# Gram matmuls of a half chunk in two blocks of two PSUM banks, and the last layer in four column tiles

## The reference

```python
e = jnp.stack([tbl_0[ids[:, 0]], ..., tbl_26[ids[:, 26]]], axis=1)    # 2048 x 27 x 128
dot_products = jnp.einsum('bnd,bmd->bnm', e, e)
z = dot_products[:, c, r]                                             # pairs below the diagonal: 351
h = jnp.concatenate([z, dense_ctx], axis=1)                           # 367
h = jnp.maximum(h @ W_top1 + b_top1, 0.0)                             # 512
h = jnp.maximum(h @ W_top2 + b_top2, 0.0)                             # 256
y = h @ W_top3                                                        # 1
```

## Time and profile before

| | us |
|---|---|
| median of 3 runs | 572.7 |
| lowest, highest | 572.4, 577.95 |
| the profiled execution | 572.74 |
| its span in the trace (first to last instruction) | 570.9 |
| mean TensorE clock granted, share of full | 0.848 |
| PE busy, PEld busy | 419.2, 367.1 |
| DVE, ACT, POOL busy | 232.5, 147.5, 253.0 |

### The profile page before, as it was taken

The page is one execution under the profiler, slowest core; times in us unless marked ns, Lnnn a source line. Parts: engine busy times, 40 slices in busy tenths (PEclk is TensorE's granted clock), DMA queues, the critical chain, the costliest instruction groups (busy, mean ns, idle before and its releaser), DMA issues.

```text
span 570.9 us, 10250 instructions
## 1 busy us (share of the span) xinstructions
PE 419.2 (73%) x4118; PEld 367.1 (64%) x4118; DVE 232.5 (41%) x730; ACT 147.5 (26%) x310; POOL 253.0 (44%) x269
## 2 busy tenths in 40 slices
PE   3411567867786896779896887858978688689887
PEld 3311566846775785658684775747867587578676
DVE  6511685524562262532462433433336225354200
ACT  3210241212221331223121331222312223124542
POOL 6777454446554443642545336254444453450000
PEclk9755588869797896978788898787979789799998
DMA  8943261234223421413215132052211431133130
GB/s 202 230 119 86 74 202 33 84 79 105 60 78 90 86 60 28 127 45 77 64 29 148 26 77 68 22 139 47 77 36 52 120 82 55 38 100 66 37 68 1
DMA packets 69280, 45.97 MB, mean 81 GB/s; under 512 B 53443, under 2 KB 57795, under 8 KB 69233
## 3 DMA queue, kind: packets, MB, share of 16 engines
q1 hardware_dynamic: 59255, 27.82, 20.4%
q0 software_dynamic: 8384, 17.19, 11.6%
q10 hardware_dynamic: 1594, 0.31, 0.3%
HBM read 39.53 MB, written 5.76 MB: 79 GB/s over the span
## 4 chain that ended last, share of the span: by engine, by line
PE 63%; issue 14%; another core or an unknown queue 11%; DVE 6%; DMA 2%; ACT 2%; SPq 1%; ACTq 0%; DVEq 0%
PE lookup_ps L558 33%; PE gram_ps L587 13%; PE layer_ps L604 7%; PE gather_ps L543 5%; DVE one_hot L833 5%; PE layer_ps L616 4%; PE layer_ps L624 1%; DMA ids_all<-lookup_ids 1%; DVE table_lo L840 1%; DMA emb<-tbl 1%; ACT z L735 1%; DMA z<-gram_dram 1%; SPq L357 1%; ACT h_rest L735 0%
## 5 line engine op out<-in xcount | busy, mean ns | idle before, releaser
L511 POOL DMA_INDIRECT rows<-tbl,index x256 | 246.4, 962 | 256.3 <-PE gather_ps L543 160.8
L833 DVE TENSOR_SCALAR one_hot<-ids_all,row_number 125x256 fp32r<-125x256 int32 x688 | 208.3, 366 | 295.0 <-remote 151.7
L558 PE MATMUL lookup_ps<-one_hot,table_hi 125*128 125x256 f32 x680 | 208.9, 332 | 86.3 <-issue 43.0
L558 PEld LDWEIGHTS lookup_ps<-one_hot,table_hi 125*128 125x128 f32 x680 | 145.6, 214 | 100.4 <-issue 65.0
L558 PE MATMUL lookup_ps<-one_hot,table_lo 125*128 125x256 f32 x680 | 193.7, 309 | 17.0 <-issue 16.7
L558 PEld LDWEIGHTS lookup_ps<-one_hot,table_lo 125*128 125x128 f32 x680 | 146.9, 216 | 26.4 <-issue 26.1
L587 PE MATMUL gram_ps<-emb 128*52 128x54 f32 x2048 | 84.4, 231 | 37.7 <-issue 35.4
L587 PEld LDWEIGHTS gram_ps<-emb 128*52 128x52 f32 x2048 | 69.8, 142 | 54.0 <-issue 47.2
L330 ACT COPY gram<-gram_ps 128x432 f32<-128x432 f32 x64 | 33.2, 518 | 193.9 <-remote 161.8
L697 ACT ACTIVATE emb<-lookup_ps 128x256 f32<-128x256 f32 x85 | 35.0, 412 | 83.8 <-remote 40.8
L686 ACT ACTIVATE emb<-gather_ps 128x512 f32<-128x512 f32 x64 | 38.9, 608 | 63.7 <-PE gather_ps L543 46.4
(11 more groups left out here) (40 smaller groups left out, 107.5 us busy)
## 6 DMA issues: line engine op xcount, KB each, us to landing
ids_all<-lookup_ids SPq DMA_DIRECT2D x43, 256.0 KB
gram_dram<-gram SPq DMA_DIRECT2D x62, 87.8 KB
emb<-tbl SPq DMA_DIRECT2D x11, 448.0 KB
rows<-tbl,index POOLq DMA_INDIRECT x256
z<-gram_dram SPq DMA_DIRECT2D x14, 117.0 KB
ids_all<-lookup_ids SPq DMA_DIRECT2D x7, 128.0 KB
z<-gram_dram SPq DMA_DIRECT2D x7, 91.0 KB
emb<-w SPq DMA_DIRECT2D x3, 192.0 KB
```

Of the source, the lines that this page charges most:

```text
L511: pool.indirect_dma_start(rows[k][:, j * DIM:(j + 1) * DIM], None, tables[f], bass.IndirectOffsetOnAxis(index[p][:, h, f:f + 1], 0)).then_ ...
L558: last = nc.tensor.matmul(lookup_ps[lookup_bank(c, p, k)], table[:, k, row, :], one_hot[u % UNIT_RING][:, r, :], start=(row == 0 and table ...
L833: last = nc.vector.tensor_scalar(one_hot[u % UNIT_RING][:, r, :], table_ids, row_number[0:LOOKUP_PARTS, row:row + 1], None, ALU.is_equal)
```

## The change

The four gram banks of a half are no longer spread singly, but in two blocks of two. A block stands at one position. `last_order()` is left as it is.

Layer three splits its 256 samples into four lots of 64. Each lot is a matmul of its own with the same weight column, and its output goes to another column tile (PSUM partitions 0, 32, 64 and 96, columns 0 to 63 of the bank). So there are eight fp32 matmuls (16 instructions) of 64 columns in place of two (four instructions) of 256. ACT's copy takes all 128 partitions by 64 columns, in place of one by 256, and the store reads four partitions of it.

```diff
+def by_blocks(events, first, end):
+
+    starts = spread([events[n:n + GRAM_BANKS] for n in range(0, len(events), GRAM_BANKS)], first, end)
+    return [(at, event) for at, block in starts for event in block]
@@ half_order
     if h == 1:
         return merged(spread([("unit", c + 1, u) for u in range(EARLY_UNITS)]), spread(gathers_of(c, 1), offset=0.6),
-                      spread(grams_of(c, 0), GRAMS_FROM, GRAMS_TO[h]))
+                      by_blocks(grams_of(c, 0), GRAMS_FROM, GRAMS_TO[h]))
     events = [spread([("unit", c, u) for u in range(EARLY_UNITS, N_UNITS)]), spread(gathers_of(c, 0), offset=0.6),
-              spread(grams_of(c - 1, 1), GRAMS_FROM, GRAMS_TO[h])]
+              by_blocks(grams_of(c - 1, 1), GRAMS_FROM, GRAMS_TO[h])]
@@ dlrm_tower
+        Y_TILES = 4
+        Y_COLS, Y_STEP = CHUNK // Y_TILES, P // Y_TILES
@@ tower
-            return Tower(z_sb, h1_sb, [h2_one, h1_sb[0]], h1_more[0:1, 0, :])
+            return Tower(z_sb, h1_sb, [h2_one, h1_sb[0]], h1_more[:, 0, 0:Y_COLS])
@@ layer3
                     pe.wait_ge(h2_ready, c * o2_tiles + k + 1)
-                    last = nc.tensor.matmul(layer_ps[0][0:1, 0:CHUNK], w3_sb[:, k:k + 1], to.h2[k],
-                                            start=(k == 0), stop=(k == o2_tiles - 1))
+                    for j in range(Y_TILES):
+                        last = nc.tensor.matmul(layer_ps[0][j * Y_STEP:j * Y_STEP + 1, 0:Y_COLS], w3_sb[:, k:k + 1],
+                                                to.h2[k][:, j * Y_COLS:(j + 1) * Y_COLS],
+                                                start=(k == 0), stop=(k == o2_tiles - 1))
                 last.then_inc(l3_full, 1)
@@ copy_y
-                nc.scalar.activation(to.y, layer_ps[0][0:1, 0:CHUNK], ACT.Copy).then_inc(y_ready, 1)
+                nc.scalar.activation(to.y, layer_ps[0][:, 0:Y_COLS], ACT.Copy).then_inc(y_ready, 1)
...
-                act.dma_start(y_out[bass.ds(c * CHUNK, CHUNK), :].rearrange("b o -> o b"),
-                              to.y).then_inc(y_stored, 16)
+                act.dma_start(y_out[bass.ds(c * CHUNK, CHUNK), :].rearrange("(j b) o -> j (b o)", j=Y_TILES),
+                              to.y[0:P:Y_STEP, :]).then_inc(y_stored, 16)
```

## The result

The changed kernel took 598.15 us (median of 4 runs, 595.98 to 599.98). The kernel before, run beside it, took 575.09 (572.4 to 577.95). The ratio is 1.040, with an interval of 1.032 to 1.048: slower by 4%, where 565.1 was forecast and 582 was the upper end of the range.

The account below looks back on a forecast made before the run. PE bounds the kernel, standing in windows of gather calls. From 572.74: odd `h == 1` +16.65, even -1.5, `h == 0` -21.3, last `h == 0` -0.8, first `h == 1` -0.3, end -0.35; together -7.6, 565.1 us; range 553 to 582.

Parts of the forecast that it names:

- the windows: Time from POOL's first gather call on: PE runs normally a while, then nearly stands until 1.0 to 2.1 us after the last.
- `h == 1` of the odd chunks: g3 to g7: blocks stand in g3's window and in the joined windows of g5 and g6; 5.55 us longer, three times.
- the even halves: `h == 1` of even chunks, g3 to g7: g4's calls stay late, 8.6 us after g3; 0.5 us shorter, three times.
- `h == 0`: g7 to L1: g7 comes when its window is over; 4.0 and 3.1 us shorter, three times each, and 0.8 at the last.
- the prediction's own list of what would make it wrong: g4's even-half signal in time (5 us lost each, three times), smaller window allowance for dense blocks, or units waiting for DVE.
- The block behind g1: Second block of `h == 0`, 18.1 to 19.9 us after g7: passes as a window opens, units behind stand, L1 at 23.75.
- Rival C: The `h == 0` block at the opening window stands in its middle: 2.85 us more in six halves, 582 us; chance 0.25.
- what a window lets through: In POOL's call windows PE first passes 48 to 52 matmuls at normal pace; grams inside a window bring the stand.
- Rival D: Stands depend on the DMAs alone, not the grams, so their sum stays; switches and layer three go: 564.7 us; chance 0.08.
- Layer three: 16 quarter-width matmuls on PE take 0.45 us where four took 0.95; 0.5 us saved each time.
- the row taken: Gram bank in the trace, two tiles of 54 columns at 28 ns a matmul, used to cost layer three at 0.45 us.
- Its store: Layer three's store, four rows of 256 bytes for one of 1 KB: costs nothing, perhaps some tenths at the end.

Follow-up runs that it names:

- the first run: The kernel before with the gram blocks alone, layer three, its copy and store as before: 594.65 us, ratio 1.029, chip P.
- the half-by-half runs: Layer three in tiles, chip R, against the kernel before: blocks in `h == 0` alone 570.18 us, ratio 1.020; in `h == 1` alone 589.54 us, 1.054.

## Why the prediction was wrong

**Right: the windows and what they do in `h == 1` of the odd chunks.** The odd timeline was forecast with g4 at 3.9 after g3, the block at 6.3, done at 14.2, g5 16.95, g6 20.7, second block 22.2, g7 34.9. Measured in chunk 3: 3.8, 6.1, 14.9, 17.2, 20.8, 22.3, 34.9. Chunks 3 and 5 lost 5.5 and 6.2 us (forecast 5.55). Blocks outside windows are 1.76 us (forecast 1.75).

**Wrong, the largest: the even halves.** They were to gain 0.5 us each, since the prediction kept the late calls of g4 (8.6 us after g3 on the chain) as they were in the kernel before, though its own shorter layer three moved g4. In the kernel before, g4's signal comes 2.8 us after the gather's end (209.30 for 206.52). In the changed kernel it comes 1.5 us after it (219.44 for 217.93) and was out before the block began at 219.74. The place of the banks is not what makes the difference. With layer three in tiles and a single bank one unit behind g4, as in the kernel before (tiles alone, and blocks in `h == 0` alone), g4 ends 4.4 us after the start of g3 and its calls begin 6.8 to 7.6 us after it in chunks 2 to 6, as in the changed kernel (6.9 to 7.0). With the old layer three and blocks (the first run) g4 ends at 5.0, and its calls begin at 8.8 in chunks 3 and 4 and at 6.7 to 6.9 in the others. The two halves with late calls took 31.2 and 33.5 us there, the other three 34.9 to 35.6. Why a signal sent 0.6 us sooner is let through sooner was not looked into.

With g4's signal in time the calls are two rows with 0.6 us between them, and that pause gives PE nothing back: the block stands through both, as if they were one. The even halves went the way of the odd ones, +4.3, +4.3 and +5.0. This is the first item in the prediction's own list of what would make it wrong, with 5 us three times as its price, but it stood in no rival and had no chance of its own. It makes 15 us of the miss of 35 (7.6 shorter was forecast, 27.3 longer came). Chunks 0 and 1, which lost 2.1 and 8.5, make 5 more, and the start, which was taken as equal, 2. Of these little can be learned: chunk 0's `h == 1` took 39.4 us in the repeat of the changed kernel and 35.4 here, and g3 of chunk 0 came at 74.2 us there and at 76.5 here.

**Wrong: `h == 0`.** It was to gain 22.1 in all and gained 10.7. One of the six halves that were to gain 3 or 4 us is chunk 0's, which has no layers; it gained nothing. In the others two terms failed. The block behind g1 was to pass in 1.8 us with the stand in the units behind it. It began 1.0 us later than forecast, since the units and the gather before it ran at the lower clock for longer (eight matmuls in 2.01 us, the gather in 0.85), and took 3.26 with stands of 0.4 us inside and behind it, so L1 came 25.7 us after g7 instead of 23.75. Layer two takes 5.2 us in the mean of chunks 1 to 5, 4.5 in the kernel before. In chunk 2 it waits for ACT's second `relu1`, which starts at 281.06, 2.5 us after the end of layer one's matmuls (278.56). They end inside a row of four calls (274.77 to 279.60), and ACT's start is 1.5 us behind that row. In the kernel before they end with the row of calls, at 265.01, and ACT starts at 265.94. That the signal stuck is argued from these times. Rival C named the stand inside the block, with L1 at 26.6. The gain itself was put down to the right thing (g7 comes when its window is over, and is signalled in time), but that is the doing of `h == 1`'s order. The blocks of `h == 0` cost time, as the half-by-half runs show.

**Wrong: what a window lets through.** It was read as a pace that units keep and gram banks don't. It is nearer to a stock, on which whatever is in the window draws. Rival D was right that the calls make the stands and not the grams, and wrong that their sum stays, since how long PE is empty in a row depends on what stood in it.

**Layer three** was costed at 0.45 and is 0.33 us on the chain; a group of eight matmuls starts 0.11 us after the other, 14 ns a matmul on average. The Trainium skill, TensorE: Matmul & The Clock Gate, Part 3, gives about 4 ns between the matmuls of a pack, by which the prediction's estimate was 0.26; the measured 0.33 lies between that and the row taken. ACT's copy takes 0.23 us in place of 0.37, as forecast. Its store was costed at nothing, with some tenths at the end as a chance, and these came: the last store takes 0.56 us to issue on ACT, where it took 0.24, and 1.54 us pass behind it to the end of the program in place of 1.36. That uses up what the shorter layer and copy save there, and the end is 0.1 us longer instead of 0.35 shorter.

**The cause.** The prediction left open what is starved. The Trainium skill, Runtime: NRT & Kernel Launch, Instruction fetch mechanics, has the fetch mostly hidden behind the sequencer. On chip Q, and with plain DMAs on chip P, the runs agree with it (PE is busy for 90% of the span). With indirect calls on chips P and R they don't: in the gram block shown PE gets six to eight instructions each 1.4 to 1.5 us. That blocks inside rows of indirect calls make the loss is shown by the runs with one edit, one half and plain DMAs. That it is the supply of instructions is argued, from PE standing with "issue" and no wait in such lots; which path the calls block was not tried, nor what differs on chip Q.

## What to carry to other kernels

Before moving instructions, lay the DMA calls of GpSimd beside PE's timeline: if PE gets its work in lots of about eight while they run, the order of calls and dense work is worth far more than entries and exits of a tiling (here 23 to 43 us against an estimated 4). Keep rows of calls short and apart, put less in each than the stock holds (28 matmuls beside four calls ran at full pace here), and let what sets off the next row wait until this one is out; a pause of 0.6 us between rows is not enough. And measure on more than one chip: an order tuned around stands that one chip has can be worth nothing, or cost 37%, on the next.

## What the runs showed of the hardware

- Indirect calls on POOL starve PE on two of three chips, plain calls (557 ns) do not, and neither do the same bytes. Release comes 1.0 us after the last of four calls, 1.6 to 2.1 after eight, 3.9 after sixteen in the rows shown. Signals stick too: up to 9.2 us to ACT, 2.8 us to POOL (g4 in chunk 2 of the kernel before).
- The same program and inputs: 374 us on chip Q, 557 to 561 on chip R, 572 on chip P, each within 1.5% of its median over seven runs. The changed kernel took 598 and 601 in two lots. It was not run as it is on chip Q; its order with a fixed list of rows took 373 there, beside 374 for the kernel before, so on that chip the change would move little.
- Over the long stands shown the mean granted clock is 0.67 to 0.82 of full. Over the short ones it is 0.98 to 1.00 (3.3 to 3.9 us; the 3.55 us of the earlier trace rows). In the kernel that keeps the rows apart it is 1.00 in the stretches shown, and 0.89 over the whole program.
